# Moving the logarithm of five gates behind their tangents in the last feed-forward stage of a decoder kernel

## The reference

```python
for _ in range(2):                                   # ITERS
    ctx = concatenate([integrated, v])
    shared_ctrl = gelu(ctx @ shared_w1 + b) @ shared_w2 + b
    ctrl_k      = the same with the expert that the router chose, for k = 1, 2
    # each ctrl splits into a, beta, g:
    v_next = sigmoid(a) * v - softplus(beta) * (integrated - mu)
    x_next = integrated + 0.1 * sigmoid(g) * v_next
    # the three (x_next, v_next) are mixed by the shared weight and the router's weights
    halt = sigmoid(gelu(integrated @ halt_w1 + b) @ halt_w2 + b)
    integrated += halt * (x_next - integrated);  v += halt * (v_next - v)
refined = gelu(integrated @ refine_w1 + b) @ refine_w2 + b
x = layernorm(x + x + integration_weight * refined)
```

## Time and profile before

| | before |
|---|---|
| median of 3 runs | 5597.75 us (5596.44 to 5598.51) |
| the profiled execution | 5598.32 us |
| its span, first to last instruction | 5596.7 us |
| mean granted clock of TensorE | 0.852 of full speed |
| TensorE busy | 4691.9 us, 84% of the span |
| VectorE busy | 2974.4 us, 53% |
| ScalarE busy | 1933.6 us, 35% |
| GpSimd busy | 1042.5 us, 19% |

### The profile page before, as it was taken

One profiled execution on the slowest core, in us unless ns is written; L12 is line 12 of the kernel. 1 busy time (PEld: TensorE's weight loads), 2 busy tenths in 40 slices (PEclk: granted clock), 3 DMA queues, 4 the chain that ended last, 5 costly groups with the idle time before them and its releaser, 6 DMA issues. The chain is left out here.

```text
span 5596.7 us, 57753 instructions
## 1 busy us (share of the span) xinstructions
PE 4691.9 (84%) x20360; PEld 2608.5 (47%) x20360; DVE 2974.4 (53%) x6224; ACT 1933.6 (35%) x3508; POOL 1042.5 (19%) x876
## 2 busy tenths in 40 slices
PE   6887899888688789988868878998886887899888
PEld 4444444543444444454344444445434444445543
DVE  5555444753655554475355555446535555544653
ACT  3243222236424322224542432222454243223245
POOL 2122100222202210022220211002222021100222
PEclk8898889869789888986979988898697998789869
DMA  2000100000100010000010001000001000100000
GB/s 77 1 3 25 54 5 2 16 1 2 51 0 3 25 54 5 2 16 1 2 50 1 3 25 54 5 3 16 1 2 50 0 3 25 54 5 3 16 1 4
DMA packets 20876, 93.08 MB, mean 17 GB/s; under 512 B 5228, under 2 KB 14444, under 8 KB 17796
## 3 DMA queue, kind: packets, MB, share of 16 engines
q1 hardware_dynamic: 20580, 89.26, 4.2%
HBM read 87.16 MB, written 2.10 MB: 16 GB/s over the span
## 5 line engine op out<-in xcount | busy, mean ns | idle before, releaser
L1314 POOL TENSOR_TENSOR arena<-arena 128x616 f32<-128x616 f32 (+1 forms) x256 | 355.0, 1387 | 1029.7 <-DVE arena L1301 1029.7
L1254 ACT ACTIVATE arena<-arena 128x616 f32<-128x616 f32 (+1 forms) x256 | 205.3, 802 | 905.9 <-DVE arena L1288 458.7
L210 POOL TENSOR_SCALAR rstd_e<-mean_var 128x4 f32<-128x4 f32 x120 | 27.4, 228 | 2428.5 <-DVE mean_var L176 2428.5
L1222 PE MATMUL ps<-const,arena 128*77 128x128 f32 (+1 forms) x2048 | 401.6, 359 | 60.4 <-POOL arena L1314 60.4
L1923 DVE TENSOR_TENSOR arena<-ps,arena 128x512 f32<-128x512 f32 x256 | 176.6, 691 | 463.5 <-ACT arena L1873 463.5
L1222 PEld LDWEIGHTS ps<-const,arena 128*77 128x77 f32 (+1 forms) x2048 | 321.4, 197 | 141.0 <-POOL arena L1314 80.5
L1873 ACT ACTIVATE arena<-ps 128x512 f32<-128x512 f32 x288 | 172.0, 597 | 602.8 <-PE ps L1821 602.8
L2263 PE MATMUL ps<-w_even,w_odd 128*128 128x512 f32 x640 | 322.9, 651 | 26.9 <-issue 26.9
L1820 PE MATMUL ps<-xT,w_even 128*128 128x512 f32 x576 | 305.3, 612 | 3.1 <-DVE arena L1910 3.1
L1827 PE MATMUL ps<-arena,w_even 128*128 128x512 f32 x576 | 294.9, 594 | 7.0 <-DVE arena L1923 4.8
L1239 PE MATMUL ps<-arena,w_even 77*32 77x128 f32 (+1 forms) x2560 | 225.5, 333 | 79.9 <-DVE arena L1308 78.4
(11 more groups left out here) (383 smaller groups left out, 9249.9 us busy)
## 6 DMA issues: line engine op xcount, KB each, us to landing
w_even<-in_w SPq DMA_DIRECT2D x4, 6916.0 KB, 19.1
w_even<-in_w SPq DMA_DIRECT2D x4, 3313.5 KB, 10.9
w_odd<-in_w SPq DMA_DIRECT2D x4, 2824.5 KB, 9.5
w_odd<-in_w SPq DMA_DIRECT2D x4, 2095.0 KB, 8.2
w_odd<-in_w SPq DMA_DIRECT2D x4, 2048.0 KB, 15.2
x_in<-in_x SPq DMA_DIRECT2D x10, 256.0 KB, 2.8
w_odd<-in_w SPq DMA_DIRECT2D x4, 577.0 KB, 3.7
w<-in_w SPq DMA_DIRECT2D x1, 2050.0 KB, 10.8
```

Of the source, the lines that this page charges most:

```text
L1222: mm = nc.tensor.transpose(ps[0:nk, 4 + h // 4, (h % 4) * P:(h % 4 + 1) * P], m["P"][u % 3][:, h, :], ident)
L1254: nc.scalar.activation(p, p, ACT.Exp, scale=scale).then_inc(c_exp.sem, 1)
L1314: nc.gpsimd.tensor_tensor(m["P"][u % 3], m["P"][u % 3], bcast(m["sum"][u % 3], m["nk"]), ALU.mult)\
```

## The change

In gates 0, 2, 5, 8 and 10 ScalarE takes the logarithm after the tangents of the same gate; in the other seven it stays between the exponential and the first tangent. The list of events of `i_act` is written in the new order, so that each wait still means the same event. TensorE, VectorE and GpSimd have the same instructions in the same order as before.

```diff
+        LN_LAST = (0, 2, 5, 8, 10)
-        i_act = signal("i_gate_functions", GATES)
+        i_act = signal("i_gate_functions", [(q, m) for q in range(12) for m in
+                                            (((2, 0, 1) if q in LN_LAST else (1, 2, 0)) if q >= 6 else
+                                             ((2, 1) if q in LN_LAST else (1, 2)))])
...
                 nc.scalar.activation(i_sp[q % 2], i_sp[q % 2], ACT.Exp, scale=-1.0)
-                nc.scalar.drain()
-                nc.scalar.activation(i_sp[q % 2], i_sp[q % 2], ACT.Ln, bias=1.0).then_inc(i_act.sem, 1)
+                if q not in LN_LAST:
+                    nc.scalar.drain()
+                    nc.scalar.activation(i_sp[q % 2], i_sp[q % 2], ACT.Ln, bias=1.0).then_inc(i_act.sem, 1)
                 act.wait_ge(i_ctl.sem, i_ctl[q, 2])
                 nc.scalar.activation(i_tg[q % 2], bank(o + 2), ACT.Tanh, scale=0.5).then_inc(i_act.sem, 1)
                 if it:
                     act.wait_ge(i_ctl.sem, i_ctl[q, 0])
                     nc.scalar.activation(i_ta[q % 2], bank(o), ACT.Tanh, scale=0.5).then_inc(i_act.sem, 1)
+                if q in LN_LAST:
+                    nc.scalar.drain()
+                    nc.scalar.activation(i_sp[q % 2], i_sp[q % 2], ACT.Ln, bias=1.0).then_inc(i_act.sem, 1)
```

## The result

Over 22 runs each in one comparison, the changed kernel took 5611.63 us (median, 5598.04 to 5628.74) and the kernel before 5599.03 us (5591.81 to 5615.55): ratio 1.0019, 95% interval 1.001 to 1.0028. By the ratio it is slower by about 0.19%, 10.6 us (the medians lie 12.6 apart): clear of zero, and near the upper end of the range. Two runs among the experiments, one of e10 (6407.07 us) and one of the kernel before in the first set (8796.40 us), lie far from all others and are left out of the ratios. The runs also spread further than before, over 30.7 us; the profiled one is the slowest, 5628.74 us with a span of 5627.1, so its totals are read round by round here, not as a sum.

What follows compares the result with a forecast made beforehand. TensorE was taken as the busiest engine, waiting on late tangents before gates 7 and 10. Per round + 1.70 - 0.55 - 0.55 = + 0.60 us, over four rounds + 2.4, gave 5600.2 us; range 5588 to 5612.

Steps and rivals of the forecast that it cites:

- The gains: Before gates 7 and 10: earlier tangents in gates 5 and 8 let each start 0.55 us earlier.
- plain sum: Moved waits at gates 4, 7 and 10, clock left out: + 1.70 - 0.55 - 0.55 = + 0.60 us a round.
- I take nothing, the nearer row's price: At gate 4: the new idle of about 1.55 us costs nothing through the clock.
- Two neighbours, 1.26 and 1.90: First-stage idles in us used to price gate 4's: four products took 1.88 us after the shorter, 3.58 after the longer.
- Rival 2: Gates 7 and 10: shrunken old idles no longer drop the clock; 5582.6 us, or 5593.5 with gate 7's alone; chance 0.12.
- Rival 3: On ScalarE: the logarithm's table also serves the exponential, ten loads a round fewer, 5600.2 us; chance 0.05.
- Rival 1: At gate 4: the new idle drops the clock, 1.67 to 2.73 us a round; + 9.1 to + 13.3 us; chance 0.30.
- Low-clock stretches move elsewhere: Elsewhere in the round: low-clock stretches moving there would make the forecast wrong; no size given.

Runs made afterwards that it cites:

- e10: Changed kernel with unread products in the idles before gates 4, 7 and 10, and layer 1's cross-attention query product made five times; 5589.53 us, ratio 0.9959.
- e9: Kernel before with unread products in the idles before gates 7 and 10, and layer 1's cross-attention query product made five times; 5588.90 us, ratio 0.9957.
- e3: Changed kernel with two unread products filling the idle before gate 4; 5638.30 us, ratio 1.0058.
- e1: Kernel before with only gate 2's logarithm moved behind the tangent; 5619.83 us, ratio 1.0031.
- e7: Kernel before with two unused VectorE additions in front of each round's last new state; 5632.54 us, ratio 1.0028.
- e2: Kernel before with only the logarithms of gates 5 and 8 moved behind the tangents; 5600.55 us, ratio 1.0.
- e11: Kernel before with gates 5 and 8's logarithms moved, unread products before gates 7 and 10, and the query product made five times; 5599.46 us, ratio 0.9978.
- e12: e9 with seven more unread products in the idle before the second refine; 5584.95 us, ratio 0.9948.
- e8: Kernel before with unread products in the old idles before gates 7 and 10; 5606.65 us, ratio 0.9993.
- e6: Kernel before with the second group's query product in layer 1's cross-attention made five times; 5613.27 us, ratio 1.0004.

## Why the prediction was right, and where not

**Right: the mechanism at each gate.** Gate 2's tangent waits for its product, gate 4 starts late, gates 7 and 10 start early, 0 and 10 are free, the loads stay at 112. From gate 1's first products to gate 4's it is 1277.98 - 1256.19 = 21.79 us after and 1276.65 - 1256.52 = 20.13 before: 1.66 late, for 1.70. The gains were 0.73 each for 0.55: gate 5's tangent starts 0.53 us behind the exponential's start, not 0.68, where the load had started. Even so the whole plain sum is small, as e10 against e9 shows.

**Wrong: "I take nothing, the nearer row's price".** The step that failed is the price of the new idle. The prediction put it at nothing; measured, the idle dropped the clock in all four rounds, at 1.8 us in three of them and 3.1 in the second (5.40 and 6.72 against 3.60). Two neighbours, 1.26 and 1.90, lay about equally far, and the choice between them decided the forecast. Both counted the idle's length alone; in front of gate 4 stand gate 3's four products of 65 rows, which neither neighbour has. The trace before has a row closer in kind that the prediction passes over, gate 1's first products behind small ones:

```profile
1255.50 1.09 PE L2241 MATMUL ps<-arena,expand 8*128 8x512 bf16 x2 [0.20 <-ACT arena L2327]
...
1256.52 6.22 PE L2263 MATMUL ps<-w_even,w_odd 128*128 128x512 f32 x8
```

There eight products take 6.22 us. The granted clock is 0.89 from 1230 to 1240 us and 0.50 from 1240 to 1256, and from 1236 to 1256 there are only products of 8 to 65 rows or of 24 columns, with no idle above 0.69 us. So the clock can fall without an idle of a microsecond; whether gate 3's light products are what tipped it at gate 4 wasn't tried, and e3's second round shows that the same idle behind the same products can go either way. e1 shows that gate 2 alone brings the cost, and e3 that the idle, not the late start, sets the clock. What the Trainium skill's page "TensorE: Matmul & The Clock Gate" (section "A second HAM failure mode: psum-queue depth-cycling") tells of short idles between groups agrees with this trace at gate 4: 1.49 us of idle, then 3.41 us at 1.2 GHz.

**Rival 2 falls, with a remainder.** The shorter old idles still dropped the clock (5.40 us behind 2.39 and 2.88, and 6.38 at gate 7 in the second round); but gate 10's price went from 2.73 to 1.70 us in all four rounds.

**Rival 3 falls.** The exponential reloads behind a logarithm 20 times, five a round. On the order logarithm, then exponential, the page "ScalarE: Activation LUTs" of the Trainium skill (section "Table sets: the hidden batching unit") says one load; here each logarithm and each exponential behind one has its own.

**Not foreseen: a second term, larger than what the gates cost.** In round 1 the stage's + 2.98 us are + 1.0 up to gate 11's last products (gate 4's start and clock, less what gates 7 and 10 win) and + 2.0 at the second refine, 1.8 of it its second four products. Rival 1 had + 2.27 to + 3.33 a round at the gates alone; that the time came out in its band is in part luck, as gate 10 got cheaper and the refine dearer. For the range the same holds: it reached this far up for rival 1's price, not for the refine. "Low-clock stretches move elsewhere" was named as what would make the forecast wrong, but not priced. And with the times of the stages the long loop comes and goes, with 7.5 to 17.4 us more in the rest of such a round. e7's profiled run has both, the dearer refine and the long loop, behind a delay without any change of order.

**What stays open.** The long loop's share in the median of the changed kernel isn't known, since only one of its runs has a profile; the stage's own cost in that run, some 14 us, is more than the measured 10.6, and the fastest runs (5598.04) are as fast as the kernel before, so some runs must win time elsewhere or pay less in the stage. Nor is it known what sets whether a given round's loop starts low, or which idles drop the clock.

## What to carry to other kernels

The sum of moved waits can be right to a third of a microsecond a round, and TensorE's clock can still decide the time: where an edit makes a new idle in front of dense products, price the low clock behind it as the likely case, and look at what runs at the low clock further on. Where rows recur round by round with low-clock stretches at fixed places, a gain of 1 us is worth testing only together with what it does to those places; here the same two gains gave nothing in e2, and e11, which has them, took 10.6 us more than e9, which hasn't. What did pay was keeping the clock up: idle TensorE time filled with products that nobody reads, together with a few dense products at a loop of small ones, took 0.4 to 0.5% off the kernel before by the ratios of the third set. Against its fastest run there e9's median is 8.6 us lower and e12's 12.6, 0.15 and 0.22%. Either of the two alone gave nothing (e8, e6).

## What the runs showed of the hardware

- A loop of small products can stay at 1.2 GHz though TensorE is busy in it without a break: 46.81 of 47.50 us busy at a granted clock of 0.50, for products of 77 and 32 rows or 77 columns; the same loop at a granted clock of 0.89 was busy 39.16 of 48.50. In 32 profiled rounds it took 65.3 us or 48.6, and nothing between.
- Busy with what doesn't matter: products of weights by weights kept the clock up as well as useful ones (3.67 to 3.70 us in all 48 filled idles before a gate, for 5.37 to 6.74 without).
- An idle of 2.39 us behind the same products was followed by the low clock in three rounds of e3 (6.74 us for eight products) and by the full clock in one (3.70).
- A delay of 1.2 us a round made the kernel slower by 3 to 29 us (95% interval) and each stage by 3.0 to 3.4, and fillers that shortened the stage by 4.2 us a round made it no faster, until the loop was dealt with (e7, e8, e9).
